# Attention and channel mixing on 8 cores: tiles 8 to 31 of the first stage transposed by DMA instead of TensorE, and their PSUM banks laid out anew

## The chip, the cores and the metric

One Trainium2 chip, all 8 cores, one launch. The metric is the device time of the slowest core in microseconds (us). The cores exchange nothing: each pair of cores has one of four sequences, each core owns half of its tokens.

## The reference, cut to what matters

```
x = x + attn(layernorm(x))      # x: 4 x 4096 x 1024, f32
x = x + ffn(layernorm(x))
attn(z): q, k, v = z @ Wq, z @ Wk, z @ Wv      # one head of width 64
         att = softmax(q @ k.T, axis=1)        # normalised over the queries i, for each key
         out = att @ v, repeated 16 times along the width
ffn(z):  xr, xk = mixes of z and z shifted by one token
         sigmoid(xr @ Wr.T) * (square(relu(xk @ Wk.T)) @ Wv.T)
```

The softmax runs over the queries. So for each tile of 128 keys the exponentials are taken over all 4096 queries, their row sums are inverted and multiplied into v, and only then can the output products for that key tile begin.

## The kernel before, in words

Each core reads all 4096 tokens of its sequence, its own 2048 first, as 32 tiles of 128 tokens (i or kt = 0..31, 512 KB each in f32). It has three stages that overlap at their edges.

**First stage.** SyncE (the SP queue, line 307) loads tile i into one of eight slots `xst`; from tile 8 on it waits until GpSimd has finished with the slot (G_Z). VectorE takes two `bn_stats` and a `bn_aggr` per tile (lines 405 to 408). GpSimd (POOL) makes the reciprocal standard deviation of two tiles at a time (lines 352 to 357) and writes the normalised tile in bf16 to one of eight slots `zst` (line 363): it adds the negated mean and multiplies. TensorE transposes the tile in eight 128x128 pieces into a PSUM bank `tb` (T(i), line 704), and ScalarE (tiles 0 to 7, line 958) or VectorE (tiles 8 to 31, line 416) copies it to `zT`. For each group n of four tiles TensorE then projects q and k (QK(n), line 713), VectorE copies them to `qk1` (line 421), TensorE swaps their halves (SW(n), line 721), VectorE copies that to `qk2` (line 425), and MX(n) (line 746) with a maximum on VectorE (line 439) gives the bound `negm` that the exponentials of these four key tiles subtract. Every second group VP projects v (line 728) and VT transposes it back (line 738), with a copy by VectorE after each (lines 429, 433).

The banks `tb0`, `tb1` of the transposes and `tf0`, `tf1` of the projections are the same two banks of PSUM under two names, and `acc`, the sum of the output, takes them over when the first stage is done. The remaining six banks are three score buffers F of two banks.

**Attention.** A unit is one key tile times 1024 queries (or 512 in the first groups): TensorE writes scores to a buffer F (`fill`, lines 759 and 763), ScalarE takes the exponential with the row sum (`exps`, line 975). There are 136 units in eight groups of 4, 8, 8, 20, 8, 16, 0 and 72; a unit of group g can begin once SW(g) has been copied, and its exponential needs the maximum of group g. 60 of the units are placed by hand between the steps of the first stage (`share`, in `scores(n, p)`), the others follow it. For each finished key tile VectorE forms `vs(kt)` = v over the row sum (line 485), and TensorE adds four products into `acc` (`out_mm`, line 771). Exponentials of own queries of key tiles 16 and up go to four rotating slots `Prot`, so tile kt can't begin before `out_mm(kt - 4)` is done. x is loaded a second time, into `x1`, which lies on the same memory as the exponentials of key tiles 0 to 15: load t waits for `out_mm(t)` (line 316). VectorE sums each of these tiles (`x_fold(t)`, line 475), in its order right after `vs(16 + t)`.

**Weights.** The three matrices of the last stage, 4 MB each in f32 and cast to bf16 on the way, lie over `xst`, `zst` and `zT`. GpSimd issues their loads (lines 372 to 376) when all 32 tiles are normalised and transposed.

**Last stage.** Residual, second layer norm, mixes and the three products of the channel mixing, in four blocks of 512 tokens. Its own transposes of tiles 5 and up are DMA transposes already, of 128x1024 bf16, issued by SyncE (line 329).

All engines run their instructions in program order, so the order written in `body` for VectorE and in the loop over `T`, `QK`, `SW`, `MX`, `VP`, `VT` and `scores` for TensorE decides who waits behind whom.

```
def body(n):
    if 4 * n + 2 >= NA:
        t_evac(4 * n + 2)
        if n % 2 == 0:
            vt_evac(n // 2 - 1)
        t_evac(4 * n + 3)
    if n < 7:
        stats(4 * n + 6)
        stats(4 * n + 7)
    qk_evac(n)
```

Of the kernel before, what the change touches and what calls it, by code (L numbers as in the profile page):

```python
# [15 lines left out]
D = 64  # L16
CT = 8
KT = 32
TT = 32
# [3 lines left out]
NA = 8  # L23
# [38 lines left out]
def build_program():  # L62
# [24 lines left out]
    for n, g in enumerate(groups):  # L87
        for u in g:
# [10 lines left out]
            ps_after.append(cnt)  # L99

    ctx = ExitStack()
    e = ctx.enter_context
    with ctx:
# [92 lines left out]
        F = [e(nc.psum_tensor(f"F{i}", [128, 1024], F32)) for i in range(3)]  # L196
# [13 lines left out]
        D_X = [sem(f"D_X{s}") for s in range(8)]  # L210
        D_R = [sem(f"D_R{t}") for t in range(TOWN)]
# [11 lines left out]
        V_T = sem("V_T")  # L223
# [48 lines left out]
        def wait_t(eng, i):  # L272
            if i < NA:
                eng.wait_ge(A_T, i + 1)
            else:
                eng.wait_ge(V_T, i - NA + 1)

        def t_bank(i):

            n, j = i // 4, i % 4  # L280
            if n == 0:
                return j % 2
            if j < 2:
                return n % 2
            return 1 if j == 2 or n % 2 == 0 else 0

# [16 lines left out]
        def _(sy):  # L303
            for i in range(TT):
# [4 lines left out]
                if i == 7:  # L309
                    sy.dma_start(out=identf[:, :], in_=idsw_in[:, 0:128]).then_inc(D_C, 16)  # L310
                    sy.dma_start(out=mu[:, :], in_=mu_in).then_inc(D_C, 16)
                    sy.dma_start(out=hmask[:, :], in_=hmask_in).then_inc(D_C, 16)
                    sy.dma_start(out=xh[:, :], in_=xh_in).then_inc(D_C, 16)
# [30 lines left out]
        def _(g):  # L344
            g.dma_start(out=idsw[:, :], in_=idsw_in).then_inc(D_ID, 16)
            g.dma_start(out=wqk[:, :, :].rearrange("p a b -> p (a b)"),
                        in_=wqk_in).then_inc(D_WQK, 16)
            g.wait_ge(V_C, 2)
            for h in range(TT // 2):
                a = 2 * h  # L350
                g.wait_ge(V_ST, 3 * (a + 2))
                g.tensor_scalar(nmean[:, a:a + 2], ag[:, a:a + 2, 0], -1.0, None,
                                ALU.mult).then_inc(G_ST, 1)
                g.tensor_scalar(vpe[:, a:a + 2], ag[:, a:a + 2, 1], EPS, None,
                                ALU.add).then_inc(G_ST, 1)
                g.wait_ge(G_ST, 3 * h + 2)
                g.tensor_tensor(rstd[:, a:a + 2], vpe[:, a:a + 2], mhalf[:, :],  # L357
                                ALU.pow).then_inc(G_ST, 1)
                g.wait_ge(G_ST, 3 * h + 3)
                for i in (a, a + 1):  # L360
                    if i >= 8:
                        g.wait_ge(P_T, i - 7)
                    g.tensor_scalar(zst[:, i % 8, :], xst[:, i % 8, :],  # L363
                                    nmean[:, i:i + 1], rstd[:, i:i + 1],
                                    ALU.add, ALU.mult).then_inc(G_Z, 1)
# [31 lines left out]
        def _(v):  # L397
# [3 lines left out]

            def stats(i):
                s = i % 4
                v.wait_ge(D_X[i % 8], 16 * (i // 8 + 1))
                v.bn_stats(bnst[:, s, 0:6], xst[:, i % 8, 0:512]).then_inc(V_ST, 1)  # L405
                v.bn_stats(bnst[:, s, 6:12], xst[:, i % 8, 512:1024]).then_inc(V_ST, 1)  # L406
                v.wait_ge(V_ST, 3 * i + 2)
                v.bn_aggr(ag[:, i, :], bnst[:, s, :]).then_inc(V_ST, 1)

            def t_evac(i):  # L410
                v.wait_ge(P_T, i + 1)
                sc = i // 8
# [30 lines left out]
            def body(n):  # L443


                if 4 * n + 2 >= NA:
                    t_evac(4 * n + 2)
                    if n % 2 == 0:
                        vt_evac(n // 2 - 1)
# [677 lines left out]
```

## Time and profile before

| what | value |
|---|---|
| median of 3 runs (lowest to highest) | 413.28 us (413.16 to 413.42) |
| the profiled execution, its own time | 413.11 us |
| its span, slowest core (core 0) | 411.5 us |
| spans of the eight cores | 406.9 to 411.5 us |
| PE, DVE, ACT, POOL busy over the span | 79%, 62%, 56%, 16% |
| first exponential to last | 31.8 to 216.4 us |

The span runs from the first to the last instruction of the core; some 1.6 us of the execution lie around it. PE is TensorE's matmuls, PEld its weight loads, DVE VectorE, ACT ScalarE, POOL GpSimd, SP SyncE, whose row in a timeline is the issuing of DMAs. DMA share is the mean busy share of the core's 16 DMA engines. "idle before <-X" names what ended the idle time in front of an instruction.

### The profile page before, as it was taken

What the parts mean: (1) busy time and instruction counts of PE and PEld (TensorE: products, weight loads), DVE (VectorE), ACT (ScalarE), POOL (GpSimd) and SP (SyncE); (2) the same over time, 40 slices, a digit from 0 to 9 for tenths busy, and PEclk for the clock granted to TensorE, in tenths of its full rate; (3) what the DMA queues carried; (4) which work ended last, traced back from release to release, by engine and by line L of the source; (5) the groups of instructions that cost most, each with busy time, mean ns of one, the idle gap of its engine ahead of it and who ended that gap; (6) DMA issues with size and microseconds to landing.
All of it is one profiled execution on the core that took longest, in us unless ns stands there. A gap on an engine that the chain in (4) does not pass through costs nothing.

```text
span 411.5 us, 5646 instructions; the slowest of 8 cores (406.9 to 411.5 us)
## 1 busy us (share of the span) xinstructions
PE 323.8 (79%) x1683; PEld 136.3 (33%) x1706; DVE 254.6 (62%) x477; ACT 230.5 (56%) x358; POOL 65.2 (16%) x94
## 2 busy tenths in 40 slices
PE   0377679677795982787772599899999999999995
PEld 0233334233331220111111444344444444444442
DVE  3737777697721434754575998688748864773036
ACT  1233275399789996899994934900491048103510
POOL 1766345554510000000000002000100000000000
PEclk9996888699877796555555599999999999999998
DMA  7995455330069999950000000413131414130014
GB/s 178 312 310 172 109 200 204 103 104 2 0 109 159 156 190 273 346 202 2 0 1 0 2 1 13 91 53 154 27 65 50 168 25 76 53 144 12 0 46 160
DMA packets 23501, 43.90 MB, mean 107 GB/s; under 512 B 14256, under 2 KB 14640, under 8 KB 23088
## 3 DMA queue, kind: packets, MB, share of 16 engines
q1 hardware_dynamic: 22608, 36.78, 28.2%
q0 software_dynamic: 864, 6.75, 10.3%
q8 instruction: 15, 0.25, 0.3%
q14 instruction: 14, 0.11, 0.1%
HBM read 38.74 MB, written 8.39 MB: 115 GB/s over the span
## 4 chain that ended last, share of the span: by engine, by line
PE 54%; DVE 13%; ACT 12%; issue 9%; DMA 9%; POOL 1%; SPq 0%; DVEq 0%; ACTq 0%; POOLq 0%
PE F L905 13%; PE F L865 10%; PE F L883 10%; PE F L759 6%; DMA x<-x_in 6%; PE tf L713 5%; PE tb L704 4%; PE acc L771 3%; ACT Prot L975 3%; DMA xst<-x_in 3%; DVE bnst L405 2%; DVE zT L416 2%; ACT junk L975 2%; DVE bnst L406 2%; PE tf L728 2%
## 5 line engine op out<-in xcount | busy, mean ns | idle before, releaser
L759 PE MATMUL F<-qk 64*128 64x512 bf16 x136 | 64.3, 486 | 22.7 <-ACT Prot L975 6.8
L763 PE MATMUL F<-qk 64*128 64x512 bf16 x120 | 58.4, 501 | 0.0
L865 PE MATMUL F<-wr,xr 128*128 128x512 bf16 x251 | 57.3, 385 | 0.4 <-issue 0.2
L905 PE MATMUL F<-wv,ka 128*128 128x512 bf16 x252 | 55.7, 379 | 2.2 <-ACT ka L1034 1.8
L1026 ACT ACTIVATE rr<-F 128x1024 bf16<-128x1024 f32 x16 | 16.4, 1023 | 72.9 <-PE F L865 72.9
L883 PE MATMUL F<-dxk,wk 128*128 128x512 bf16 x249 | 55.5, 379 | 0.6 <-issue 0.2
L975 ACT ACTIVATE P<-F,negm 128x1024 bf16<-128x1024 f32 (+1 forms) x40 | 37.3, 948 | 28.8 <-PE F L759 23.3
L704 PE MATMUL tb<-idsw,zst 128*128 128x128 bf16 x256 | 23.4, 246 | 26.4 <-POOL zst L363 16.8
L975 ACT ACTIVATE junk<-F,negm 128x1024 bf16<-128x1024 f32 x32 | 37.1, 1174 | 5.5 <-PE F L763 5.4
L975 ACT ACTIVATE Prot<-F,negm 128x1024 bf16<-128x1024 f32 x32 | 36.7, 1198 | 5.4 <-PE F L763 5.4
L363 POOL TENSOR_SCALAR zst<-xst,nmean,rstd 128x1024 bf16<-128x1024 f32 x32 | 38.1, 1198 | 4.0 <-POOL rstd L357 3.7
L651 DVE TENSOR_TENSOR tmp<-F,rr 128x1024 f32<-128x1024 f32 x15 | 18.4, 1224 | 31.5 <-PE F L905 31.3
L759 PEld LDWEIGHTS F<-qk 64*128 64x128 bf16 x136 | 12.5, 97 | 75.2 <-issue 73.6
L975 ACT ACTIVATE junkL<-F,negm 128x1024 bf16<-128x1024 f32 x32 | 37.2, 1186 | 0.0
L865 PEld LDWEIGHTS F<-wr,xr 128*128 128x128 bf16 x256 | 25.5, 100 | 30.8 <-issue 1.9
L905 PEld LDWEIGHTS F<-wv,ka 128*128 128x128 bf16 x256 | 24.9, 98 | 32.1 <-issue 2.3
L883 PEld LDWEIGHTS F<-dxk,wk 128*128 128x128 bf16 x256 | 25.0, 98 | 30.6 <-issue 0.7
L475 DVE TENSOR_REDUCE xf<-x 128x64 f32<-128x1024 f32 x16 | 30.1, 1890 | 6.6 <-DMA x<-x_in 6.6
L713 PE MATMUL tf<-zT,wqk 128*128 128x512 bf16 x57 | 23.5, 582 | 9.7 <-ACT zT L958 3.6
L704 PEld LDWEIGHTS tb<-idsw,zst 128*128 128x128 bf16 x256 | 17.6, 109 | 35.6 <-issue 35.6
L556 DVE SCALAR_TENSOR_TENSOR xr<-dxk,mu,z1T 128x256 bf16<-128x256 bf16 (+1 forms) x72 | 27.2, 450 | 2.3 <-PE F L865 1.1
L405 DVE BATCH_NORM_STATS2 bnst<-xst 128x6 f32<-128x512 f32 x32 | 21.7, 678 | 7.8 <-DMA xst<-x_in 7.8
(102 smaller groups left out, 395.5 us busy)
## 6 DMA issues: line engine op xcount, KB each, us to landing
xst<-x_in SPq DMA_DIRECT2D x32, 512.0 KB, 5.3
x<-x_in SPq DMA_DIRECT2D x16, 512.0 KB, 23.9
y_out<-x SPq DMA_DIRECT2D x15, 512.0 KB, 2.6
wr<-wr_in POOLq DMA_DIRECT2D x1, 2048.0 KB, 17.9
wk<-wk_in POOLq DMA_DIRECT2D x1, 2048.0 KB, 30.9
wv<-wv_in POOLq DMA_DIRECT2D x1, 2048.0 KB, 44.9
y_out<-x SPq DMA_DIRECT2D x2, 256.0 KB, 2.0
wqk<-wqk_in POOLq DMA_DIRECT2D x1, 256.0 KB, 10.6
```

What stands on the lines that cost most here:

```text
L363: g.tensor_scalar(zst[:, i % 8, :], xst[:, i % 8, :], nmean[:, i:i + 1], rstd[:, i:i + 1], ALU.add, ALU.mult).then_inc(G_Z, 1)
L405: v.bn_stats(bnst[:, s, 0:6], xst[:, i % 8, 0:512]).then_inc(V_ST, 1)
L475: v.reduce_sum(xf[:, t_, :], x1[:, t_, :].rearrange("p (j d) -> p d j", d=D), axis=AX.X).then_inc(V_XF, 1)
L556: ins = v.scalar_tensor_tensor(xr[:, ct, o:o + w], dxk[:, q % 2, ct, o:o + w], mu[:, ct:ct + 1], z1T[:, ct, c0 - 1:c0 + w - 1], ALU.mult, ...
L704: ins = t.transpose(tb[t_bank(i)][:, ct, :], zst[:, i % 8, ct * 128:(ct + 1) * 128], ident)
L713: ins = t.matmul(tf[n % 2][:, :], wqk[:, ct, :], zT[:, (n // 2) % 2, ct, (n % 2) * 512:(n % 2 + 1) * 512], start=(ct == 0), stop=(ct == CT ...
L759: t.matmul(f[:, 0:512], qk2[0:64, kt * 128:(kt + 1) * 128], qk1[0:64, i0:i0 + 512], start=True, stop=True, skip_group_check=True, tile_pos ...
L763: t.matmul(f[:, 512:1024], qk1[64:128, kt * 128:(kt + 1) * 128], qk2[64:128, i0 + 512:i0 + 1024], start=True, stop=True, skip_group_check= ...
L865: ins = t.matmul(f[:, hh * 512:(hh + 1) * 512], xr[:, ct, j * 128:(j + 1) * 128], wr[:, ct, hh * 512:(hh + 1) * 512], start=(ct == 0), sto ...
L883: ins = t.matmul(F[k_ % 3][:, dd * 512:(dd + 1) * 512], wk[:, ct, dt * 128:(dt + 1) * 128], dxk[:, q % 2, ct, :], start=(ct == 0), stop=(c ...
L905: ins = t.matmul(F[(8 + j) % 3][:, hh * 512:(hh + 1) * 512], ka[:, dt, j * 128:(j + 1) * 128], wv2[:, dt, hh * 512:(hh + 1) * 512], start= ...
L975: sc.activation(dst, F[u_ % 3][:, 0:w], AF.Exp, bias=negm[:, kt:kt + 1], accum_out=ellp[:, ell_col[u_]:ell_col[u_] + 1]).then_inc(A_EXP, 1)
```

## The change

Tiles 0 to 7 are transposed by TensorE as before, now into banks `tx` of their own (they lie under the third score buffer F2), and copied by ScalarE. Tiles 8 to 31 are transposed by SyncE's DMA, directly from `zst` to `zT`. In SyncE's order the transpose of tile i is followed by the load of tile i + 8. VectorE has no copies of tiles any more. The projections have two banks, `tf0` for QK and MX, `tf1` for SW, VP and (as `tb1`) VT. Until unit 20 the scores have two buffers, from then on three. MX(n) for n > 0 uses the upper halves of `qk1` and `qk2` and no longer waits for the copy of SW(n). GpSimd makes the statistics of tiles 8 to 31 four tiles at a time, and issues the load of `wqk` only after tile 1 of x has landed. The orders on VectorE and TensorE are written out, with `bn_stats` of a tile between the copies of q/k and of the swap, and 65 units in the first stage where there were 60. The weight loads wait for the last eight DMA transposes. The shift by the negated mean in `apply` is the same instruction as before.

```
-NA = 8
+NPT = 8
+NF2 = 20
...
+    f_of = [u % 2 if u < NF2 else (u - NF2 + 2) % 3 for u in range(NU)]
+    f_prev = [max([p for p in range(u) if f_of[p] == f_of[u]], default=-1) for u in range(NU)]
...
-        F = [e(nc.psum_tensor(f"F{i}", [128, 1024], F32)) for i in range(3)]
+        F = [e(nc.psum_tensor(f"F{i}", [128, 1024], F32)) for i in range(2)]
+        tx_cm = [nc.psum_tensor(f"tx{i}", [128, 8, 128], BF16) for i in range(2)]
+        tx = opens(tx_cm)
+        closes(tx_cm)
+        F.append(e(nc.psum_tensor("F2", [128, 1024], F32)))
...
@@ sync
+            for i in range(TT):
+                if i >= NPT:
+                    sc = i // 8
+                    sy.wait_ge(G_Z, i + 1)
+                    if i % 8 == 0 and sc >= 2:
+                        sy.wait_ge(P_QK, 2 * (sc - 2) + 2)
+                        sy.wait_ge(P_V, 2 * (sc - 2) + 2)
+                    sy.dma_start_transpose(
+                        out=zT[:, sc % 2, :, (i % 8) * 128:(i % 8 + 1) * 128],
+                        in_=zst[:, i % 8, :]).then_inc(D_ZT[i % 8], 16)
+                if i + 8 < TT:
+                    load_x(i + 8)
...
@@ gpsimd
+            g.wait_ge(D_X[1], 16)
             g.dma_start(out=wqk[:, :, :].rearrange("p a b -> p (a b)"),
                         in_=wqk_in).then_inc(D_WQK, 16)
...
+            def apply(i):
+                if NPT <= i - 8:
+                    g.wait_ge(D_ZT[i % 8], 16 * (i // 8 - 1))
+                elif i >= 8:
+                    g.wait_ge(P_T, i - 7)
+                g.tensor_scalar(zst[:, i % 8, :], xst[:, i % 8, :],
+                                nmean[:, i:i + 1], rstd[:, i:i + 1],
+                                ALU.add, ALU.mult).then_inc(G_Z, 1)
...
+            for n in range(2, 8):
+                scale(4 * n, 4, n + 2)
+                for i in range(4 * n, 4 * n + 4):
+                    apply(i)
             g.wait_ge(G_Z, TT)
-            g.wait_ge(P_T, TT)
+            for i in range(TT - 8, TT):
+                g.wait_ge(D_ZT[i % 8], 16 * (i // 8))
...
@@ vector (n is the group; stats(i) = stats_a(i), stats_b(i))
+            for i in range(9):
+                stats(i)
+            qk_evac(0)
+            stats_a(9)
+            sw_evac(0)
+            stats_b(9)
+            mx(0)
+            for i in range(10, 14):
+                stats(i)
...
+            qk_evac(3)
+            stats_a(18)
+            sw_evac(3)
+            mx(3)
+            stats_b(18)
+            stats(19)
+            stats(20)
+            stats(21)
+            v_evac(1)
+            stats(22)
+            vt_evac(1)
+            stats(23)
+            qk_evac(4)
...
+            qk_evac(5)
+            stats_a(26)
+            sw_evac(5)
+            mx(5)
+            stats_b(26)
+            stats(27)
+            v_evac(2)
+            stats(28)
+            vt_evac(2)
+            stats(29)
+            stats(30)
+            stats(31)
+            qk_evac(6)
...
@@ tensor
             def QK(n):
-                wait_t(t, 4 * n + 3)
-                if n >= 2 and n % 2 == 0:
-                    t.wait_ge(V_VT, n // 2)
+                if n == 0:
+                    t.wait_ge(D_WQK, 16)
+                if n < 2:
+                    t.wait_ge(A_T, 4 * n + 4)
+                else:
+                    for i in range(4 * n, 4 * n + 4):
+                        t.wait_ge(D_ZT[i % 8], 16 * (i // 8))
+                if n >= 1:
+                    t.wait_ge(V_MX, n)
...
-            share = [0, 4, 8, 8, 10, 10, 10, 10]
...
+            QK(3)
+            scores(2)
+            SW(3)
+            MX(3)
+            scores(1)
+            VP(1)
+            scores(3)
+            VT(1)
+            scores(7)
+            QK(4)
+            scores(3)
+            SW(4)
+            MX(4)
+            scores(4)
+            QK(5)
```

## Rows read from the trace of the kernel before

**Rows 1.** The chain of work that ended last: start, us, what.
```profile
137.41 24.16 DMA x<-x_in
```
**Rows 2.** Timeline of DVE, 150 to 165 us: start, us, instruction, idle before.
```profile
155.57 1.88 DVE L475 TENSOR_REDUCE xf<-x 128x64 f32<-128x1024 f32 x1 [3.02 <-DMA x<-x_in]
...
161.66 1.87 DVE L475 TENSOR_REDUCE xf<-x 128x64 f32<-128x1024 f32 x1 [3.54 <-DMA x<-x_in]
```
**Rows 3.** Timelines of POOL and of SP around the end of the first stage.
```profile
114.66 0.62 POOL L372 DMA_DIRECT2D wr<-wr_in  x1 [4.25 <-PE tb L704]
...
115.80 0.55 POOL L376 DMA_DIRECT2D wv<-wv_in  x1
...
135.87 29.87 SPq L316 DMA_DIRECT2D x<-x_in  x16
```
**Rows 4.** The page's DMA issues: KB each, us from issue to landing.
```profile
x<-x_in SPq DMA_DIRECT2D x16, 512.0 KB, 23.9
...
wv<-wv_in POOLq DMA_DIRECT2D x1, 2048.0 KB, 44.9
```
**Rows 5.** Stretches, line 975 (exponentials) only: ACT busy, PEclk, DMA share, GB/s.
```profile
30.00:118.00 88.00, 53.12 (x106) 0.81 0.36 110
...
168.00:217.00 49.00, 48.73 (x90) 0.50 0.25 90
```
**Rows 6.** Timeline of ACT: the first exponential of the last group.
```profile
131.68 1.15 ACT L975 ACTIVATE junkL<-F,negm 128x1024 bf16<-128x1024 f32 x1
```
**Rows 7.** Whole stretches: PE, PEld, DVE, ACT, POOL busy, PEclk, DMA share, GB/s.
```profile
14.00:118.00 104.00, 75.82 (x489) 36.69 (x496) 73.46 (x138) 61.03 (x114) 55.31 (x79) 0.84 0.46 142
```
**Rows 8.** Groups of instructions by line, 0 to 135 us: busy, mean ns, idle before.
```profile
L363 POOL TENSOR_SCALAR zst<-xst,nmean,rstd 128x1024 bf16<-128x1024 f32 x32 | 38.1, 1198 | 4.0 <-POOL rstd L357 3.7 <-PE tb L704 0.2
...
L405 DVE BATCH_NORM_STATS2 bnst<-xst 128x6 f32<-128x512 f32 x32 | 21.7, 678 | 7.8 <-DMA xst<-x_in 7.8
...
L416 DVE COPY zT<-tb 128x1024 bf16<-128x1024 bf16 x24 | 16.3, 684 | 8.9 <-PE tb L704 8.9
...
L421 DVE CAST qk<-tf 128x512 bf16<-128x512 f32 x8 | 5.5, 688 | 12.2 <-PE tf L713 12.2
```
**Rows 9.** Timeline of DVE: starts of two tiles' statistics that follow each other.
```profile
31.35 0.67 DVE L405 BATCH_NORM_STATS2 bnst<-xst 128x6 f32<-128x512 f32 x1
...
32.84 0.67 DVE L405 BATCH_NORM_STATS2 bnst<-xst 128x6 f32<-128x512 f32 x1
```
**Rows 10.** Timeline of PE: starts of QK(3), QK(4), QK(5).
```profile
61.87 2.99 PE L713 MATMUL tf<-zT,wqk 128*128 128x512 bf16 x7 [2.33 <-DVE zT L416]
...
77.25 3.19 PE L713 MATMUL tf<-zT,wqk 128*128 128x512 bf16 x7 [0.89 <-ACT P L975]
...
89.72 1.67 PE L713 MATMUL tf<-zT,wqk 128*128 128x512 bf16 x7 [0.76 <-ACT P L975]
```
**Rows 11.** Timeline of POOL: the step to tiles 8 and 9.
```profile
33.08 0.23 POOL L352 TENSOR_SCALAR nmean<-ag 128x2 f32<-128x2 f32 x1 [4.68 <-DVE ag L408]
...
34.71 2.38 POOL L363 TENSOR_SCALAR zst<-xst,nmean,rstd 128x1024 bf16<-128x1024 f32 x2 [0.24 <-POOL rstd L357]
```
**Rows 12.** One line's instructions: ns minimum/median/maximum, first and last start, forms.
```profile
L357 POOL TENSOR_TENSOR rstd<-vpe,mhalf x16: 697/708/732, 10.5 to 107.1; 128x2 f32<-128x2 f32 x16
...
L384 POOL TENSOR_TENSOR rstd<-vpe,mhalf x2: 850/1651/2452, 251.1 to 259.5; 128x8 f32<-128x8 f32 x1, 128x3 f32<-128x3 f32 x1
```
**Rows 13.** The same for the DMA transposes of the last stage, and us to landing.
```profile
L329 SPq DMA_TRANSPOSE z1T<-z x11: 1232/1232/1327, 255.3 to 344.6; - x11
...
z1T<-z SPq DMA_TRANSPOSE x11, 3.1
```
**Rows 14.** Stretches: a lone DMA transpose; few loads; the loads of most of the stage.
```profile
256.00:259.00 3.00, 3.00 (x15) 1.35 (x15) 2.90 (x12) 2.91 (x4) 0.00 (x0) 1.00 0.47 87
45.00:50.00 5.00, 2.05 (x11) 0.99 (x13) 4.20 (x10) 1.05 (x4) 3.03 (x5) 0.75 0.12 49
35.00:90.00 55.00, 41.44 (x266) 19.36 (x269) 41.42 (x78) 28.27 (x61) 28.01 (x41) 0.82 0.50 154
```

More of the change, by code:

```diff
@@ L210, in build_program @@
         D_X = [sem(f"D_X{s}") for s in range(8)]
+        D_ZT = [sem(f"D_ZT{s}") for s in range(8)]
         D_R = [sem(f"D_R{t}") for t in range(TOWN)]
@@ L303, in _, with load_x @@
         def _(sy):
-            for i in range(TT):
+            def load_x(i):
                 if i >= 8:
@@ L467, in _ @@
-            for i in range(6):
-                stats(i)
-            for n in range(8):
-                body(n)
+            for i in range(9):
+                stats(i)
+            qk_evac(0)
[5 more added lines that the diff above has]
+                stats(i)
+            qk_evac(1)
+            stats_a(14)
+            sw_evac(1)
+            mx(1)
+            stats_b(14)
+            stats(15)
+            v_evac(0)
@@ new lines, in _ @@
+            vt_evac(0)
+            qk_evac(2)
+            stats_a(16)
+            sw_evac(2)
+            mx(2)
+            stats_b(16)
+            stats(17)
+            qk_evac(3)
[11 more added lines that the diff above has]
+            qk_evac(4)
+            stats_a(24)
+            sw_evac(4)
@@ new lines, in _ @@
+            mx(4)
+            stats_b(24)
+            stats(25)
+            qk_evac(5)
[11 more added lines that the diff above has]
+            qk_evac(6)
+            sw_evac(6)
+            mx(6)
+            qk_evac(7)
+            sw_evac(7)
+            mx(7)
+            v_evac(3)
@@ L737, in VT @@
                 for m in range(4):
[L738 removed]
+                    ins = t.transpose(tb[1][:, m, :],
                                       vT[:, sc % 2, m * 128:(m + 1) * 128], ident)
                 ins.then_inc(P_VT, 1)
[L742 to L750 removed]
             def fill(u_):
@@ L775, in out_mm, with scores @@
                              tile_position=(0, 64 * half)).then_inc(P_O, 1)
-            share = [0, 4, 8, 8, 10, 10, 10, 10]
             begun = 0
-            def scores(n, p):
+            def scores(n):
                 nonlocal begun
-                while begun < sum(share[:n]) + (p + 1) * share[n] // 8:
+                for _ in range(n):
                     fill(begun)
@@ L790, in _ @@
             T(1)
[L791 to L815 removed]
+            T(2)
+            T(3)
+            QK(0)
+            T(4)
+            T(5)
+            SW(0)
+            T(6)
+            MX(0)
+            scores(1)
+            T(7)
+            scores(1)
+            QK(1)
+            scores(2)
+            SW(1)
+            MX(1)
+            scores(1)
+            VP(0)
+            scores(2)
+            VT(0)
+            scores(3)
+            QK(2)
+            scores(2)
+            SW(2)
+            MX(2)
+            scores(6)
+            QK(3)
+            scores(2)
+            SW(3)
+            MX(3)
+            scores(1)
+            VP(1)
[3 more added lines that the diff above has]
+            QK(4)
+            scores(3)
+            SW(4)
+            MX(4)
+            scores(4)
+            QK(5)
+            scores(3)
+            SW(5)
+            MX(5)
+            scores(1)
+            VP(2)
+            scores(3)
+            VT(2)
+            scores(8)
+            QK(6)
+            scores(3)
+            SW(6)
+            MX(6)
+            scores(3)
+            QK(7)
+            scores(3)
+            SW(7)
+            MX(7)
+            scores(1)
+            VP(3)
+            scores(2)
             VT(3)
```

204 lines of the change are left out of this document (66 added, 138 removed).

## The prediction

> **What bounds the kernel now.** I read the end first. In the chain of waits the longest single piece is not compute but a load: one of x, waited for over 24 us [rows 1]. The timeline of VectorE shows how it bites: the tile sums `x_fold(0)` and `x_fold(1)` begin at 155.57 and 161.66 us, both released by a landing [rows 2]. `vs(17)` and `vs(18)` stand behind them, `out_mm(17)` and `out_mm(18)` behind those, and the four `Prot` slots then stop the exponentials. From `x_fold(1)` to the last exponential (216.4 us) it is 54.7 us, and ScalarE is busy for 48.7 of the last 49 us [rows 5], so nothing after that landing can be shortened by an earlier first stage.
>
> Why does x land so late? The weights are issued from 114.66 us, when the last tile is transposed; the last matrix, issued at 115.80, takes 44.9 us and lands at 160.7 [rows 3, 4]. The x loads, issued from 135.87, share the DMA engines with them: the first takes 19.7 us, the second lands 6.1 us later, just after the last weight. So x tile 1 lands 47.0 us after the first weight issue. **The date that sets the end is W, the first weight issue**, that is, when all 32 tiles are normalised and transposed.
>
> Ahead of W no engine is full: from 14 to 118 us VectorE is busy 73.5 of 104 us, TensorE 75.8, DMA 0.46 [rows 7]. Exponentials fill only 53 of 88 us [rows 5], and the last group begins at 131.68 [rows 6]. The stage is a loop of waits: statistics, normalise, transpose, copy, QK, copies, statistics again. QK(3), QK(4), QK(5) begin at 61.9, 77.25 and 89.7 [rows 10].
>
> **The change, part by part.**
>
> *VectorE.* 24 copies of 0.684 us go: 16.3 us of work, and 8.9 us of waiting for TensorE ahead of them [rows 8]. One tile's statistics take 1.49 us from start to start [rows 9], so four tiles with copies of q, swap and maximum cost about 6.0 + 3 x 0.69 + 0.6 for v = 8.7 us per group instead of 11.4. This is no gain by itself: in program order `qk_evac(n)` still stops VectorE until QK(n) is done, and what QK(n) waits for is new.
>
> *TensorE.* 192 transposes go. They ran in time in which it waited; I price them at nothing. If that cover were gone they would be some 0.6 to 1 us per tile. The side effect is a lower clock: QK takes about 1.7 us at the full granted clock and 3.2 at half [rows 10]; ahead of the new QK(3) and QK(5) TensorE waits, so I take 3.1 and 2.4.
>
> *GpSimd.* Normalising stays at 1.20 us per tile [rows 8]; the addition of the negated mean is already there, so that part of the title changes nothing. Statistics to the first z are 1.63 us from the first small operation to line 363 [rows 11], with 0.71 of it the power on two columns. On four columns it isn't in the trace; on 3 and 8 columns it takes 0.85 and 2.45 [rows 12]. Between these ends I take 1.1, nearer to three columns. With the semaphore that makes 2.2 us from the last statistics of a batch to the start of its first tile. `wqk`, issued behind tile 1, lets tiles 2 and 3 land earlier (nothing to 1.5 us; I take 0.5). Its cover is that QK(0) needs it only at 22 us; were that gone QK(0) would slip by a microsecond or two.
>
> *SyncE and DMA, the heart of it.* A DMA transpose of 128x1024 bf16 takes 1.23 us to issue and 3.1 to land [rows 13]; a lone one keeps the 16 engines busy for 0.47 x 3 = 1.41 us [rows 14]. That the two queue up behind each other is the point: the change puts load i + 8 between transposes i and i + 1 of one queue. A load costs 0.12 x 5 us for 0.47 tile = 1.28 us where few run, and 0.50 x 55 us for 16.2 tiles = 1.70 us over most of the stage [rows 14]. How long it is beside transposes isn't in the trace; I take 1.5, the middle, because half as many loads per time collide as in the 1.70 row, though never as few as in the 1.28 row. A pair then costs 2.9 us of DMA, while GpSimd delivers a tile every 1.2 us. The transposes of a batch are therefore late not by 3.1 us, but by the batch. No row shows a transpose behind a load, so its own delay is open from 3.1 us (none) to the full queue.
>
> The Trainium skill says otherwise of the price: "Advanced Engine Details and Errata", section X-Bar Transpose (TRN2), has transposes as fast as regular DMAs, 350 to 400 GB/s. At 375 this tile would be an estimated 0.70 us. The row of this case, 262 KB in 1.41 us or 186 GB/s, speaks against it for this shape.
>
> **The walk.** z of tile 8 was finished at 34.7 + 1.2 = 35.9 [rows 11]; +0.4 for the power, -0.5 for the start: 35.8. The transpose reaches the DMA engines 1.3 us after its issue, at 37.2. From there eight transposes and seven loads stand back to back (tiles 12 to 15 are normalised by 47.4, long before their turn): 8 x 1.41 + 7 x 1.5 = 21.8, and 0.4 to the semaphore. QK(3) begins at 59.4 (before 61.9). Then QK 3.1, the copies, maximum and statistics up to tile 19 4.9, batch 2.2, tile 1.2, issue and start 1.4: transpose 16 is at the engines at 72.2. In VectorE's new order tiles 20 to 23 follow at once, so again eight and seven stand in the queue: QK(5) begins at 72.2 + 22.2 = 94.4 (before 89.7); QK(4) in between at about 83 (before 77.3). From QK(5): 2.4 for it; VectorE's qk copy, half statistics, swap copy and maximum 2.4, half and tile 27 2.4, v copy with its wait 1.4, tile 28 1.5, vt 0.5, tiles 29 to 31 4.5, which is 12.7 less 0.5 of overlap; batch 2.2, four tiles 4.8, last transpose 3.1. Sum 24.7. **W = 119.1, against 114.7: 4.4 us later.** After tile 23 no loads are left, so these transposes are not queued.
>
> The exponentials gain: 38 units are begun by QK(5) and 53 before QK(6) at about 112; after it, at 115.6, eleven units of 1.09 us lead to the last group at about 128 instead of 131.7. The x loads then begin 4 us earlier, at 132.2, which is W + 13 instead of W + 21. x tile 0 lands 19.7 us later, at W + 33; tile 1 has more time beside the weights and lands between W + 42 and W + 47; I take W + 44.6 = 163.7. That is 2.0 us behind 161.7, and the end follows it one for one. The last stage is as before. The profiled execution took 413.11 us, the median is 413.28: 413.1 + 2.0 + 0.2 = **415.3 us**.
>
> **The rivals.**
>
> *B, faster: the transposes hardly queue.* If loads and transposes overlap in the engines, each transpose lands about 3.1 us after its issue. QK(3) is then at 54 (held by the two score buffers), QK(5) at 80, W at 104.7, 14.4 us earlier than in the walk: 401 us. Half of it gives some 408. For it: the lone 3.1 us [rows 13], an average DMA share of only 0.46 [rows 7]. Against: one queue for both, and 1.41 us each. It decides once a pair costs less than about 2.3 us of DMA. The skill's price of 0.70 would take 16 x 0.71 = 11.4 us from the walk and end here, at 404. The skill also says ("DMA: Bandwidth & Descriptors", Queues, rings and completion order) that each engine consumes a ring's descriptors in order, which speaks for the queue; no row shows it for a transpose.
>
> *C, slower still: the loads keep their 1.70 us and x gains nothing from its earlier start.* W is 2.8 later, and x tile 1 stays at W + 47: 420 us.
>
> *D, faster: the end isn't tied to the weights.* If x lands in time for the earlier exponentials, the end moves with the last group by 4 us: 409. Against it are 19.7 us beside the weights with only 20 to 25 to spare.
>
> **How the numbers follow.** The walk (A) 0.57, B 0.25, C 0.10, D 0.08. A's own range is 411 to 419: 14 loads between 1.28 and 1.70 are -3 to +3 us, QK's clock and the power 1 to 2, x tile 1 -2.6 to +2.4. A measurement of this kernel tells some 0.2% (0.8 us) from no change; of A a fifth is faster than that, a fifth within it, three fifths slower. Faster: 0.11 + 0.25 + 0.08 = 0.44; within 0.11; slower 0.34 + 0.10, about 0.45. As cases of both signs hold the chance, the range takes in most of B and C: 402 to 420.
>
> **What would show it.** Right: DMA share near 1 from 37 to 59 and from 72 to 94 us; transposes of tiles 11, 15, 19, 23 landing 6 to 15 us after their issue; QK(4) and QK(5) released by a DMA, and VectorE idle ahead of `qk_evac(4)`; first weight issue near 119; the last group near 128; `x_fold(1)` near 164 and still released by a landing. Wrong: transposes of 3 to 4 us to landing and W under 112 (B); an end without a wait for x (D). A weight issue at 119 with an end under 412 would refute the tie between W and the end.

## The result and the profile after

The changed kernel takes 423.23 us (median of 4, 422.45 to 424.17); the kernel before beside it takes 413.22 us. The ratio is 1.024, with a 95% interval of 1.0223 to 1.0256: slower by 10 us, where 2 us were forecast and the range ended at 420. The profiled execution took 423.24 us with a span of 421.4 us. Some executions of any of these kernels run with one die at a lower clock and are several per cent longer; the medians given for the kernels of the experiments leave these out.

Of the page of the changed kernel: the span, the busy times, the clock and the DMA share in 40 slices, and the issues that answer to [rows 4, 13].

```profile
span 421.4 us, 5236 instructions; the slowest of 8 cores (415.7 to 421.4 us)
PE 315.2 (75%) x1514; PEld 124.1 (29%) x1514; DVE 238.7 (57%) x453; ACT 230.1 (55%) x358; POOL 60.1 (14%) x76
...
PEclk9996668576768696575555569999999999999999
DMA  7997990993488999991000000413131315040004
...
x<-x_in SPq DMA_DIRECT2D x16, 512.0 KB, 30.2
```

The work that was taken away is visibly gone: in the stretch from 14 to 118 us VectorE is busy 54.2 us instead of 73.5 and TensorE 60.9 instead of 75.8 [rows 7]. Nothing came of it. Whole stretches of the changed kernel, with the columns of [rows 7]:

```profile
14.00:118.00 104.00, 60.91 (x282) 21.70 (x280) 54.20 (x109) 59.91 (x113) 46.02 (x56) 0.73 0.75 188
37.00:60.00 23.00, 14.90 (x57) 4.57 (x57) 9.38 (x18) 10.87 (x25) 8.22 (x9) 0.65 1.13 256
75.00:97.00 22.00, 9.10 (x37) 2.70 (x35) 6.13 (x12) 14.05 (x27) 7.63 (x9) 0.66 1.12 265
65.00:70.00 5.00, 4.21 (x27) 1.55 (x25) 4.58 (x10) 3.55 (x7) 0.23 (x1) 0.95 0.00 0
```

The DMA engines are full in two bursts (the share sums the times of the packets, which can overlap, so it can pass 1) and empty between them; VectorE, in the second burst, works 6.1 of 22 us, and right between the bursts 4.6 of 5. They take turns instead of running together. TensorE's granted clock is 0.65 and 0.66 in the bursts, in which it is busy 14.9 of 23 and 9.1 of 22 us, and 0.95 between them, where it is busy 4.2 of 5. The waits say who waits for whom. Waits of the stretch 0 to 136 us: engine, line, releaser, us in total, times, longest.

```profile
POOL nmean L362 <- DVE ag L433: 55.1, 9, 23.6
DVE qk L441 <- PE tf L756: 47.6, 6, 13.4
...
PE tf L756 <- DMA zT<-zst: 16.3, 5, 6.7
```

It is a ring: the transposes wait for GpSimd, GpSimd for VectorE's statistics, VectorE stands in program order behind `qk_evac`, that waits for QK, and QK for the transposes. In the kernel before VectorE waited 12.2 us in front of the same copy [rows 8], now 47.6. The timeline of PE, line 756, shows QK(2), QK(3), QK(4), QK(5), QK(6); it answers to [rows 10]:

```profile
49.61 3.57 PE L756 MATMUL tf<-zT,wqk 128*128 128x512 bf16 x8 [4.52 <-DMA zT<-zst]
60.69 3.57 PE L756 MATMUL tf<-zT,wqk 128*128 128x512 bf16 x8 [0.71 <-DMA zT<-zst]
86.48 3.32 PE L756 MATMUL tf<-zT,wqk 128*128 128x512 bf16 x8 [6.70 <-DMA zT<-zst]
97.45 3.57 PE L756 MATMUL tf<-zT,wqk 128*128 128x512 bf16 x8 [2.17 <-DMA zT<-zst]
118.07 3.57 PE L756 MATMUL tf<-zT,wqk 128*128 128x512 bf16 x8 [2.19 <-DMA zT<-zst]
```

QK(5) is 7.7 us later than before. The SP and POOL timelines, which answer to [rows 3, 11, 12]: a transpose at the start and in the middle of a burst, the last eight, GpSimd's power on four columns, the first weight, and the loads of x.

```profile
35.53 1.34 SPq L317 DMA_TRANSPOSE zT<-zst  x1
...
73.07 1.24 SPq L317 DMA_TRANSPOSE zT<-zst  x1
...
80.21 2.85 SPq L317 DMA_TRANSPOSE zT<-zst  x1
...
110.25 13.12 SPq L317 DMA_TRANSPOSE zT<-zst  x8
139.94 36.30 SPq L324 DMA_DIRECT2D x<-x_in  x16
```

```profile
70.42 1.03 POOL L367 TENSOR_TENSOR rstd<-vpe,mhalf 128x4 f32<-128x4 f32 x1
...
115.76 4.72 POOL L377 TENSOR_SCALAR zst<-xst,nmean,rstd 128x1024 bf16<-128x1024 f32 x4 [0.24 <-POOL rstd L367]
125.77 0.62 POOL L396 DMA_DIRECT2D wr<-wr_in  x1 [5.29 <-DMA zT<-zst]
```

W is 125.77 us, 11.1 later than before. From there the end follows. VectorE's timeline, `x_fold(0)` and `x_fold(1)` [rows 2], and ScalarE's, the first exponential of the last group [rows 6] and the last one:

```profile
159.11 1.88 DVE L528 TENSOR_REDUCE xf<-x 128x64 f32<-128x1024 f32 x1 [2.43 <-DMA x<-x_in]
...
171.75 1.86 DVE L528 TENSOR_REDUCE xf<-x 128x64 f32<-128x1024 f32 x1 [10.08 <-DMA x<-x_in]
```

```profile
135.77 1.13 ACT L1062 ACTIVATE junkL<-F,negm 128x1024 bf16<-128x1024 f32 x1
...
225.36 1.38 ACT L1062 ACTIVATE junkL<-F,negm 128x1024 bf16<-128x1024 f32 x1
```

The table puts the dates of the slowest core beside each other for both kernels and for the experiments of the next section. In all eight in which x was waited for, `x_fold(1)` begins 45.8 to 47.7 us after W, and the last exponential 53.5 to 53.8 us after that. The profiled execution of a_late was the longest of its ten (415.73 us), so its dates are some 3 us late against its median.

| kernel | median us | W | x_fold(1) | last group | last exp. begins |
|---|---|---|---|---|---|
| before | 413.2 | 114.7 | 161.7 | 131.7 | 215.4 |
| after | 423.2 | 125.8 | 171.8 | 135.8 | 225.4 |
| b_wlate | 422.1 | 122.8 | 170.5 | 131.4 | 224.0 |
| b_defer | 407.3 | 115.2 | no wait | 132.2 | 209.7 |
| b_split | 407.3 | 115.3 | no wait | 131.2 | 208.7 |
| a_defer | 412.3 | 126.4 | no wait | 136.6 | 214.0 |
| a_late | 413.0 | 118.6 | 164.4 | 128.8 | 217.9 |
| a_pairs | 412.4 | 114.2 | 160.9 | 123.2 | 214.6 |
| a_lp | 407.1 | 108.6 | 155.2 | 117.1 | 209.0 |
| a_half | 419.3 | 123.5 | 169.7 | 134.0 | 223.4 |
| a_ahead | 416.1 | 117.5 | 164.0 | 125.0 | 217.7 |
| a_lpd | 394.1 | 109.3 | no wait | 118.4 | 195.8 |
| a_best | 395.9 | 110.5 | no wait | 121.2 | 198.5 |

### The profile page after: what moved, and what is told of

Its sections match the earlier page's. It is cut to its first block, busy times and chain, and to the rows that moved or that the text cites. A ratio compares the mean times of both kernels' runs of the same rounds, so it can differ in the third digit from the quotient of the medians.

```text
span 421.4 us, 5236 instructions; the slowest of 8 cores (415.7 to 421.4 us)
## 1 busy us (share of the span) xinstructions
PE 315.2 (75%) x1514; PEld 124.1 (29%) x1514; DVE 238.7 (57%) x453; ACT 230.1 (55%) x358; POOL 60.1 (14%) x76
## 3 DMA queue, kind: packets, MB, share of 16 engines
q1 hardware_dynamic: 47952, 43.08, 36.8%
## 4 chain that ended last, share of the span: by engine, by line
PE 45%; DMA 16%; DVE 10%; ACT 9%; issue 8%; SPq 8%; POOL 3%; DVEq 0%; ACTq 0%; POOLq 0%
PE F L992 12%; PE F L952 10%; PE F L970 10%; DMA x<-x_in 7%; SPq L317 6%; DMA xst<-x_in 6%; PE F L814 5%; DMA zT<-zst 3%; PE tf L756 3%; PE acc L826 3%; ACT Prot L1062 2%; SPq L301 2%; DVE xr L609 2%; ACT junk L1062 2%; ACT z L1090 1%
## 5 line engine op out<-in xcount | busy, mean ns | idle before, releaser
L952 PE MATMUL F<-wr,xr 128*128 128x512 bf16 x256 | 58.7, 390 | 0.0
L756 PE MATMUL tf<-zT,wqk 128*128 128x512 bf16 x64 | 26.2, 583 | 18.9 <-DMA zT<-zst 16.3
L1062 ACT ACTIVATE junkL<-F,negm 128x1024 bf16<-128x1024 f32 x32 | 37.2, 1181 | 0.0
L970 PEld LDWEIGHTS F<-dxk,wk 128*128 128x128 bf16 x256 | 25.0, 98 | 30.2
L441 DVE CAST qk<-tf 128x512 bf16<-128x512 f32 x8 | 5.5, 685 | 47.6 <-PE tf L756 47.6
L428 DVE BATCH_NORM_STATS2 bnst<-xst 128x6 f32<-128x512 f32 x32 | 21.8, 681 | 10.4 <-DMA xst<-x_in 10.4
L826 PE MATMUL acc<-Prot,vs 128*64 128x512 bf16 x64 | 15.8, 590 | 15.8 <-DVE vs L538 15.8
## 6 DMA issues: line engine op xcount, KB each, us to landing
x<-x_in SPq DMA_DIRECT2D x16, 512.0 KB, 30.2
```

The source lines that it names most:

```text
L756: ins = t.matmul(tf[0][:, :], wqk[:, ct, :], zT[:, (n // 2) % 2, ct, (n % 2) * 512:(n % 2 + 1) * 512], start=(ct == 0), stop=(ct == CT - 1 ...
L826: t.matmul(acc[64 * half:64 * half + 64, (w % 2) * 512:(w % 2 + 1) * 512], vs[:, kt * D:(kt + 1) * D], own_p(kt)[:, w * 512:(w + 1) * 512] ...
L952: ins = t.matmul(f[:, hh * 512:(hh + 1) * 512], xr[:, ct, j * 128:(j + 1) * 128], wr[:, ct, hh * 512:(hh + 1) * 512], start=(ct == 0), sto ...
L970: ins = t.matmul(F[k_ % 3][:, dd * 512:(dd + 1) * 512], wk[:, ct, dt * 128:(dt + 1) * 128], dxk[:, q % 2, ct, :], start=(ct == 0), stop=(c ...
L1062: sc.activation(dst, F[f_of[u_]][:, 0:w], AF.Exp, bias=negm[:, kt:kt + 1], accum_out=ellp[:, ell_col[u_]:ell_col[u_] + 1]).then_inc(A_EXP, 1)
```

## The experiments

Differences to the changed kernel are those of the medians; by the ratios they are up to 1 us larger.

The theory: W sets the end through the weights, and W is late because transposes and loads share one queue and a batch of four waits for its last tile. The rivals: the end comes later through the later last group, not through W; or the queue costs little and the batch, or VectorE's order, all of it. No run takes apart the rest of the change (the new banks, two score buffers until unit 20, MX without the swap, 65 units instead of 60); what these parts give or cost stays open.

**b_wlate: the kernel before, only W later.** Nothing of the first stage is changed but the date of the weight issue.

```
             g.wait_ge(P_T, TT)
+            g.wait_ge(V_MX, 8)
             g.dma_start(out=wr[:, :, :].rearrange("p a b -> p (a b)"),
```

> The kernel before the change with one wait added: GpSimd issues the weights only after the last maximum (V_MX at 8), at about 122.7 us instead of 114.7. Nothing else is touched. Theory Q: x tile 1 lands 44.6 to 46 us after W, near 168 instead of 161.7, and the whole is 6 to 7 us longer, 419 to 420 us. Rival E (the end depends on the work of the first stage, not on the weights' date): 413 us, within 1 us.

Measured: 422.06 us, ratio 1.0186 [1.0171, 1.0201]. W is 8.1 us later, the last group where it was, and the last exponential 8.6 us later. The tie is shown, and it is one for one. The x loads, which begin as early as before and so nearer to W, gained x tile 1 nothing: `x_fold(0)` is only 1.4 us later than before, `x_fold(1)` 8.8 us. That is why the whole is 2 us above the 419 to 420 that were expected. Timelines of POOL and DVE of this kernel:

```profile
122.78 0.62 POOL L373 DMA_DIRECT2D wr<-wr_in  x1 [11.83 <-DVE negm L440]
```

```profile
156.97 1.87 DVE L476 TENSOR_REDUCE xf<-x 128x64 f32<-128x1024 f32 x1 [4.74 <-DMA x<-x_in]
170.46 1.86 DVE L476 TENSOR_REDUCE xf<-x 128x64 f32<-128x1024 f32 x1 [10.94 <-DMA x<-x_in]
```

**a_defer and b_defer: the tie cut in both kernels.** `wk` and `wv2` are issued only once `out_mm(15)` is done; the last stage needs them much later.

```
             g.dma_start(out=wr[:, :, :].rearrange("p a b -> p (a b)"),
                         in_=wr_in).then_inc(D_WR, 16)
+            g.wait_ge(P_O, 4 * TOWN)
             g.dma_start(out=wk[:, :, :].rearrange("p a b -> p (a b)"),
```

> The changed kernel with the loads of the second and third weight matrix held back until out_mm(15) is done (P_O at 64), so that the second load of x meets one matrix only. Theory Q (the end is tied to x tile 1, which lands when the weights do): VectorE no longer waits for x, exponentials run through from 135.8 and end near 215 instead of 226.7, the whole 411 to 413 us although the first stage is as late as before. Rival E: the end stays at 421 to 424 us, because the late first stage itself costs the 10 us.

> The kernel before the change with only the second and third weight matrix held back until out_mm(15). Theory Q: the first stage and the start of the last group (131.7) stay, the wait for x tile 1 goes, the last exponential begins 77.4 us after the last group's first (as in a_defer) at 209 instead of 215.4; the whole 406 to 408 us. Then the changed kernel with the same edit (a_defer, 412.3) is still 4 to 6 us slower than this one, which is what the later last group costs by itself. Rival E: no change, 413 us.

Measured: the changed kernel with it 412.28 us, 0.9953 [0.9936, 0.997]; the kernel before with it 407.25 us, 0.9844 [0.9827, 0.9862]. By their pages x lands in a median of 12.0 and 11.2 us instead of 30.2 and 23.9, and no `x_fold` waits. VectorE's timeline of the changed kernel so edited, the first two `x_fold` without a wait:

```profile
157.23 1.90 DVE L529 TENSOR_REDUCE xf<-x 128x64 f32<-128x1024 f32 x1
159.72 1.90 DVE L529 TENSOR_REDUCE xf<-x 128x64 f32<-128x1024 f32 x1
```

In both, the last exponential begins 77.5 us after the first of the last group. So with the tie gone the end hangs on the last group, and the change still costs 5.0 us: its last group begins 4.4 us later. The cost of the change is thus not only the collision with the weights. The first stage itself is slower.

**b_split: is it one matrix or the total?** In the kernel before, `wk` is issued as ever and only `wv2` is held back, by the same wait.

```
                         in_=wk_in).then_inc(D_WK, 16)
+            g.wait_ge(P_O, 4 * TOWN)
             g.dma_start(out=wv2[:, :, :].rearrange("p a b -> p (a b)"),
```

> The kernel before the change with only the third weight matrix held back until out_mm(15); the second stays where it is. Theory Q (x tile 1 lands when the last weight that was issued ahead of it lands): two matrices are through 31 us after W, near 146, x tiles 0 and 1 before 152, so the wait goes as in b_defer; the whole 406.5 to 408 us. Rival F (x tile 1 needs a fixed 26 us from its own issue at 137, whatever the weights): the wait for x stays, 412 us or more.

Measured: 407.33 us, 0.9858 [0.9834, 0.9881], the same as b_defer. One matrix (2 MB in bf16) less beside the x loads is enough: `wk` lands 30.3 us after its issue, the x loads take a median of 21.8 us, and none is waited for. In the eight kernels that wait, x tile 1 lands 0.2 to 0.9 us after the last weight, though its own issue is anything from 12 to 23 us after W; here, with `wk` the last one ahead of it, it lands at 148.3 us, 2.0 us after `wk`. Why it lands with the last weight and not earlier stays open.

**a_late: loads moved out of the bursts.** The loads of x keep their number and size, but none stands between the transposes of a batch.

```
-                if i + 8 < TT:
-                    load_x(i + 8)
+                for j in {0: [8], 1: [9], 2: [10], 3: [11], 4: [12], 5: [13],
+                          6: [14], 7: [15], 11: [16, 17],
+                          15: [18, 19, 20, 21, 22, 23], 19: [24, 25],
+                          23: [26, 27, 28, 29, 30, 31]}.get(i, []):
+                    load_x(j)
```

> The changed kernel with nothing but the place of the x loads in SyncE's queue altered: loads 16 and 17 follow transpose 11, loads 18 to 23 transpose 15, 24 and 25 transpose 19, 26 to 31 transpose 23. Theory Q (transposes are late because they stand in one queue with the loads, and the date W of the first weight issue sets the end): transposes land 3 to 4 us after issue, QK(3) at 54 instead of 60.7, QK(5) at 81 instead of 97.5, W near 109 instead of 125.8, x tile 1 near 155, the whole near 407 us, below the kernel before. Rival P (a DMA transpose is itself slow beside anything else in this stage, the order in the queue doesn't matter): QK(3) and QK(5) within 3 us of their places, 420 to 423 us. Rival E (the end is set by the supply of scores or TensorE's lower granted clock): W moves, the end does not, 420 us or more.

Measured: 412.97 us, 0.9972 [0.9953, 0.999], 10 us under the changed kernel. On the slowest core QK(2) begins at 45.46 us instead of 49.61 and QK(4) at 81.01 instead of 86.48; on the seven others W is 110.4 to 113.7. The direction is theory Q's, the size is not: on those seven W is 1 to 5 us after its 109, and the whole stays 6 us above its 407. What holds the slowest core back is new: tile 18 is now loaded late, and VectorE waits for it. Its timeline on that core:

```profile
63.27 0.69 DVE L431 BATCH_NORM_STATS2 bnst<-xst 128x6 f32<-128x512 f32 x1 [3.75 <-DMA xst<-x_in]
```

**a_pairs: GpSimd's statistics two tiles at a time.**

```
-            for n in range(2, 8):
-                scale(4 * n, 4, n + 2)
-                for i in range(4 * n, 4 * n + 4):
+            for n in range(4, 16):
+                scale(2 * n, 2, n)
+                for i in range(2 * n, 2 * n + 2):
```

> The changed kernel with GpSimd's statistics of tiles 8 to 31 made two tiles at a time, as before the change, instead of four. Theory Q: each burst of transposes starts 3 to 4 us earlier, the DMA queue stays the limit inside a burst; QK(3) near 57, QK(5) near 91, and the last transpose lands 3 us sooner after the last statistics; W near 116, the whole near 414 us. Rival P or E: W near 122 or an end that does not follow it, 420 us or more.

Measured: 412.42 us, 0.9959 [0.9946, 0.9973], 11 us under the changed kernel. It doubles the number of small GpSimd operations and still gains, since tiles 16 and 17 no longer wait for the statistics of 18 and 19, which stand behind QK(3): transposes 16 and 17 are issued at 57.18 and 59.14 us instead of 73.07 and 75.04, only 18 and 19 wait until 70.17 and 72.14, and QK(4) begins at 77.89 instead of 86.48. The first transpose, of tile 8, is issued at 31.18 instead of 35.53. SyncE's timeline of this kernel, transposes 16 and 18:

```profile
57.18 1.24 SPq L317 DMA_TRANSPOSE zT<-zst  x1
...
70.17 1.26 SPq L317 DMA_TRANSPOSE zT<-zst  x1
```

**a_lp and a_lpd: both, and both with the weights held back.** The edits are those of a_late and a_pairs; a_lpd adds that of a_defer.

> The changed kernel with both edits of the first call: x loads behind the bursts of transposes (as a_late) and statistics in pairs (as a_pairs). Theory Q: QK(3) near 53, QK(5) 75 to 79, W 101 to 105, x tile 1 46.5 us after it, last exponential 53.6 us after that, the whole 399 to 404 us. If the two edits remove the same wait: W about 110, 411 us, as each alone.

> As a_lp, and the second and third weight matrix held back until out_mm(15). Theory Q: with the tie to the weights gone the supply of scores is the bound: last group begins near 118, its exponentials run through for 77.4 us, the whole 393 to 397 us. If the wait for x was not what a_lp still pays, 399 us or more.

Measured: a_lp 407.13 us, 0.9841 [0.9824, 0.9858]; a_lpd **394.11 us, 0.9534 [0.9502, 0.9566]**. The two causes overlap: 10 and 11 us alone, 16 together. The 407.1 lies between the two forecasts for a_lp, since W is 108.6 and not 101 to 105. With the tie cut the rest shows: 19 us under the kernel before. Some 6 of these the kernel before gains too by the same cut; against b_defer it is 13 us. Moving loads 18 and 19 forward to tile 11 as well (a_lpd2) gave 395.05 us, 0.9559 [0.9536, 0.9582], no gain over it.

> As a_lpd, but loads 18 and 19 stand behind transpose 11 and not behind transpose 15 (in a_late one core waited 3.75 us for tile 18 at 63 us). Theory Q: transposes 12 to 15 land up to 3 us later, the wait for tile 18 goes; within 2 us of a_lpd, either way.

**a_ahead: VectorE's order alone.** In the changed kernel the statistics of tiles 16 and 17 stand ahead of `qk_evac(2)`, those of 18 and 19 ahead of `qk_evac(3)`, and likewise 24 to 27 ahead of `qk_evac(4)` and `qk_evac(5)`.

```
             vt_evac(0)
+            stats(16)
+            stats(17)
             qk_evac(2)
-            stats_a(16)
             sw_evac(2)
             mx(2)
-            stats_b(16)
-            stats(17)
+            stats(18)
+            stats(19)
             qk_evac(3)
```

> The changed kernel with only VectorE's order altered: statistics of tiles 16 and 17 stand ahead of the copy of QK(2), 18 and 19 ahead of that of QK(3), 24 and 25 ahead of that of QK(4), 26 and 27 ahead of that of QK(5), where it idled 6 to 13 us. Theory Q (in program order the next burst's statistics wait for the projection that waits for the last burst's transposes): transpose 16 issues near 63 instead of 73, QK(4) near 77, QK(5) near 92, W near 116, the whole 412 to 415 us. Rival (the bursts' DMA time alone sets QK(5), the gaps between them are not on the path): W within 3 us of 125.8, 420 us or more.

Measured: 416.08 us, 1.0069 [1.0051, 1.0087], 7 us under the changed kernel, and just above the 412 to 415 that were expected. Transpose 16 is issued at 63.04 instead of 73.07 us, QK(4) begins at 76.84 without a wait. But QK(5) then waits for the queue. The timeline of PE of this kernel, QK(4) and QK(5):

```profile
76.84 3.58 PE L752 MATMUL tf<-zT,wqk 128*128 128x512 bf16 x8
90.52 3.57 PE L752 MATMUL tf<-zT,wqk 128*128 128x512 bf16 x8 [4.18 <-DMA zT<-zst]
```

**a_half: half of each transpose.** Only the first 512 columns of a tile are transposed by DMA; QK and VP of tiles 8 to 31 read that half twice, so the output lacks the second half of the width.

```
-                        out=zT[:, sc % 2, :, (i % 8) * 128:(i % 8 + 1) * 128],
-                        in_=zst[:, i % 8, :]).then_inc(D_ZT[i % 8], 16)
+                        out=zT[:, sc % 2, 0:4, (i % 8) * 128:(i % 8 + 1) * 128],
+                        in_=zst[:, i % 8, 0:512]).then_inc(D_ZT[i % 8], 16)
```

> The changed kernel with DMA transposes of the first 512 of the 1024 columns only (half the packets), everything else in place: the projections of groups 2 to 7 read these columns twice, so the output lacks the second half of the width. It prices the transposes themselves. Theory Q: a pair of transpose and load costs the DMA 0.7 to 0.8 us less, QK(3) 5 to 6 us earlier than 60.7, QK(5) 11 to 13 us earlier than 97.5, W near 113, the whole 410 to 412 us. Rival L (the loads alone fill the queue): QK(5) within 4 us of its place, 419 us or more.

Measured: 419.3 us, 1.0121 [1.0091, 1.0152], 4 to 5 us under the changed kernel. This was a miss: the time and the place of QK(5) are those named for rival L, and it shows where my walk was built wrong. Half the transposed bytes hardly move QK(2): it begins at 49.0 us in the mean of the cores, against 49.4. QK(5) begins at 93.5 in the mean, against 96.4. The timeline of PE on the slowest core, QK(2) to QK(5), says why:

```profile
50.87 2.92 PE L756 MATMUL tf<-zT,wqk 128*128 128x512 bf16 x7 [5.24 <-DMA zT<-zst]
60.76 3.28 PE L756 MATMUL tf<-zT,wqk 128*128 128x512 bf16 x8
87.46 3.19 PE L756 MATMUL tf<-zT,wqk 128*128 128x512 bf16 x7 [8.41 <-DMA zT<-zst]
96.47 3.57 PE L756 MATMUL tf<-zT,wqk 128*128 128x512 bf16 x8
```

QK(3) and QK(5) wait for no DMA here, and follow QK(2) and QK(4) by 9.9 and 9.0 us, which is the copies, the score units and SW and MX between them in program order. The long waits stand ahead of QK(2) and QK(4). These hang on four transposes only, and on this core the fourth lands as late as before: transposes 8 to 11 take a median of 5.1 us and at most 6.7 to land, against 5.9 and 6.8 with whole tiles. In the mean of the cores the way from the first transpose's issue to QK(2) is 13.2 us instead of 14.4, and from transpose 16 to QK(4) 12.8 instead of 13.8; the first burst also starts 0.7 us later here, so QK(2) keeps 0.4 of the 1.1. So beside loads half the bytes give back some 0.3 us for each of four transposes. Without loads they give 0.8 us to landing. The trace of line 317 from 109 to 112.5 us, transposes 24 to 26, where no load is in the queue, half tiles:

```profile
DMA to landing us min/median/max: 2.4/2.5/2.5
```

The same three in the changed kernel, whole tiles, from 110 to 114 us:

```profile
DMA to landing us min/median/max: 3.2/3.2/3.2
```

Part of the gain is capped by SyncE itself: where a half transpose takes 1.20 us to issue, the pair with its load still comes every 1.9 us. The share of DMA from 35 to 60 us did fall (mean over the cores 1.09 to 0.87), about what half the bytes are worth, but the date did not follow. In the whole burst the changed kernel moves 256 GB/s, where loads alone move 313 GB/s in the kernel before from 10 to 30 us. From the first issue to QK(2) the slowest core of the changed kernel takes 14.1 us (13.4 from transpose 16 to QK(4)), that of a_late, with no load between the four transposes, 9.8. Taking out the loads is worth more there than halving the transposes; why transposes between loads land so late stays open.

**a_best: everything together**, with the loads of a_late spread more evenly (16 to 19 after transpose 11, 20 to 23 after 15, 24 to 27 after 19, 28 to 31 after 23), pairs, the weights held back and VectorE's order ahead.

> All edits together: loads 16 to 19 behind transpose 11, 20 to 23 behind 15, 24 to 27 behind 19, 28 to 31 behind 23; statistics in pairs; two weight matrices held back until out_mm(15); VectorE's order as in a_ahead. Theory Q: below a_lpd (394.1) by the earlier last group: it begins at 112 to 115 instead of 115 to 118, the whole 389 to 392 us. If the score units' places in TensorE's order are the bound by now: 394 us.

Measured: 395.9 us, 0.956 [0.9518, 0.9603]; the intervals of a_lpd and a_best overlap. W is 110.5 against 109.3 in a_lpd. The forecast of 389 to 392 us was missed, and its alternative of 394 by 2. On top of pairs and late loads VectorE's order showed no gain; it was not run there by itself, since the loads stand otherwise too. No version is clearly better than a_lpd.

## Why the prediction was wrong

**The mechanism held.** The end is tied to W (shown by b_wlate and by a_defer), the stretch from `x_fold(1)` to the last exponential is unchanged (53.8 us before, 53.6 after), the DMA share is over 1 in both bursts, VectorE idles ahead of `qk_evac(4)` for 13.45 us, QK(4) and QK(5) are released by a DMA, and x tile 0 is folded at W + 33.3 (W + 33 forecast). The power on four columns took 1.03 us where I took 1.1. Rival B, transposes that hardly queue, is out: they land in a median of 5.5 us, and W is not under 112. Rival D is out too: the second `x_fold` waits 10.08 us. Rival C was nearest, 420 us, with one of its two reasons: x gained nothing from its earlier start, but the loads did not cost 1.70 us each. One sign did not come as written: transposes 11, 15, 19 and 23 were to land 6 to 15 us after their issue and took 6.8, 5.9, 6.0 and 4.8. The queue shows in their issue instead, which SyncE stretches from 1.23 to up to 2.85 us.

**The step that failed is the sizes of the terms of the walk to W: 119.1 forecast, 125.8 measured, and the tile that was to gain on W.** The terms, on the slowest core:

| step | forecast | measured | off |
|---|---|---|---|
| transpose 8 at the engines | 37.2 | 36.8 (issue 35.53 + 1.3) | -0.4 |
| from there to QK(3) | 22.2 | 23.9 | +1.7 |
| QK(3) to transpose 16 at the engines | 12.8 | 13.7 | +0.9 |
| from there to QK(5) | 22.2 | 23.1 | +0.9 |
| QK(5) to W | 24.7 | 28.3 | +3.6 |
| W to `x_fold(1)` | 44.6 | 46.0 | +1.4 |

They add up to 8.1 us, and 415.3 + 8.1 is 423.4.

*QK(5) to W, +3.6.* Two terms. QK took 3.57 us at a granted clock of 0.50, the lower of TensorE's two levels, where I had taken 2.4 as a mean of both levels: TensorE had waited ahead of each QK from QK(2) to QK(6), and all of them ran at half the clock but for part of QK(4), at 0.56. That is 1.2. Part of it is a misreading: [rows 10] hold only seven of the eight matmuls of a QK (x7); eight take 3.57 us at 0.50, and QK(1) of this core took 1.89 at 1.00. The same misreading makes 0.5 of the +0.9 behind QK(3), priced at 3.1. The last transpose was priced at 3.1 us from [rows 13], a lone one, and W came 5.3 us after the last z (120.48). That is 2.2. I wrote that "these transposes are not queued", since no loads were left. They queue in SyncE's issuing: the issue of the transpose ahead took 2.16 us, and the last is issued at 122.1 though its z was ready at 120.48. From there it lands in 3.2 us, as a lone one does, and W follows 0.4 us later. The trace of line 317, durations of issue (min/median/max ns) and landing:

```profile
L317 SPq DMA_TRANSPOSE zT<-zst x24: 1232/1704/2851, 35.5 to 122.1; - x24
...
DMA to landing us min/median/max: 3.2/5.5/6.9
```

*The bursts, +1.7 and +0.9.* The pair cost 2.7 us (35.53 to 54.56 for seven pairs), less than the 2.9 of the walk, so the total came out nearly right, by luck. But its structure was wrong. I counted eight transposes and seven loads back to back up to QK(3). In the trace QK(3) waits only 0.71 us for DMA, on three cores not at all; it is QK(2) that waits, for transpose 11, which was issued at 42.58 and released it 7.0 us later. QK(3) then comes by program order behind QK(2), 11.1 us on this core and 10.1 to 10.9 on the others. Two chains of nearly the same length ran side by side, and I had priced one. That is why a_half, which shortens mostly the one I had priced (its eight transposes are issued in 15.2 us instead of 19.0, mean of the cores), moved QK(5) by 3 us and not by the 11 to 13 I had put on record.

*x tile 1, +1.4.* I let it gain 2.4 us since the x loads were to begin at W + 13 and not at W + 21; they begin at W + 14.2. It gains nothing: 46.0 us after W here and 47.7 in b_wlate, against 47.0 before. It lands with the last weight. The price of that wait was also overstated at the start: the 24 us of [rows 1] are the load's own time, and VectorE waits 3.0 and 3.5 us of it [rows 2].

**What I had left out.** The walk took batches of four and the interleaved loads as given, and asked what they cost on top of the old schedule. The runs show what they are worth by themselves: 10 us for the loads in the queue, 11 us for the batch of four, 7 us for statistics behind `qk_evac`. They overlap and don't add up. The saving that the change was built on, 16.3 us of VectorE's copies [rows 8], does not show at the end. VectorE had slack before (busy 73.5 of 104 us) and waits longer now; that the copies had only filled waits is my reading, which no run tests by itself.

On the chip's own price of a transpose: a lone one moved 186 GB/s [rows 14], and the bursts, loads and transposes together, 256 and 265 GB/s at a share over 1. The Trainium skill, "Advanced Engine Details and Errata", section X-Bar Transpose (TRN2), gives 350 to 400 GB/s; no stretch here with transposes comes near it, and the measurement decides. The Trainium skill's "DMA: Bandwidth & Descriptors", section Latency and other measured facts, gives 261 GB/s for a transpose whose output is not contiguous in its middle dimension, as this one's is; that is nearer to the bursts, though they hold loads too and so don't measure it.

## What to carry to other kernels

A transpose moved from a compute engine to DMA is best kept out from behind loads that nobody needs yet, and its producer should not hold tiles back for a batch when they wait for different things: here those two choices were worth 16 us together, about as much as all the work of the copies. Before pricing a new wait, follow every chain to the instruction it holds: the fourth transpose and the program order behind it mattered here, more than the eighth. And look once at large transfers that are issued early out of habit: holding back one 2 MB weight until its stage was near gave 6 us in the kernel before by one line, and with two held back the gains of the repaired first stage reached the end (394.11 us, 4.7% under the kernel before, 13 us under that kernel with the same two held back).

## What the runs showed of the hardware

- A DMA transpose of 128x1024 bf16 lands 3.1 us after its issue alone [rows 13], but in 4.7 to 6.9 us when loads of 512 KB stand between (3.3 for the first of the second burst), and its issue on SyncE stretches from 1.23 to up to 2.85 us. These are the slowest core's.
- Transposes of half the size land in 2.4 to 2.5 us instead of 3.2 where no load is in the queue (24 to 26). Between loads they lower the DMA share (1.09 to 0.87), but the first four take nearly as long to land (median 5.1 against 5.9 us on the slowest core), and a pair of transpose and load is issued every 2.2 instead of 2.7 us.
- A 512 KB load issued 7 us earlier relative to three weight loads of another queue landed no earlier relative to them (its `x_fold` 45.8 to 47.7 us after the first weight, in all eight kernels in which it was waited for). With one of the three held back it was no longer waited for.
- GpSimd's power on 4 columns takes 1.03 us, between 0.85 for 3 and 2.45 for 8 [rows 12].
- A QK of eight 128x512 matmuls takes 3.57 us at a granted clock of 0.50 and 1.89 at 1.00.
